# The causal triangle of attention's second pass: from TensorE's sums to a copy on ScalarE, an add on GpSimd and a later exponential

## What is computed

```python
att = jnp.einsum('bthd,bsd->bhts', q, k) * scale
causal = jnp.tril(jnp.ones((Tlen, Tlen), dtype=bool))   # a token sees itself and earlier ones
att = jnp.where(causal[None, None], att, -jnp.inf)
att = jax.nn.softmax(att, axis=-1)
y = jnp.einsum('bhts,bsd->bthd', att, v).reshape(Bsz, Tlen, C)
```

## Time and profile before

| | us |
|---|---|
| median of 3 runs | 1453.11 |
| lowest, highest | 1449.94, 1455.83 |
| the profiled execution, its time | 1456.77 |
| its span, first to last instruction | 1455.5 |
| second passes of attention, from the first exponential to the last weighing | 704 to 1445 |

### The profile page before, as it was taken

One profiled execution on the slowest core, in us unless ns is written; L12 is line 12 of the kernel. 1 busy time (PEld: TensorE's weight loads), 2 busy tenths in 40 slices (PEclk: granted clock), 3 DMA queues, 4 the chain that ended last, 5 costly groups with the idle time before them and its releaser, 6 DMA issues.

```text
span 1455.5 us, 27738 instructions
## 1 busy us (share of the span) xinstructions
PE 1321.3 (91%) x10444; PEld 602.2 (41%) x10444; DVE 1136.2 (78%) x2765; ACT 880.3 (60%) x1177; POOL 498.3 (34%) x449
## 2 busy tenths in 40 slices
PE   5889997898999988789999999999999999999987
PEld 2224232323242323345544455544446545454433
DVE  5698699749887966689888898777886978877734
ACT  2686986687878766432455555555554556455564
POOL 5642453236226241740044340053520254400043
PEclk8799999999999999789999999999999999999998
DMA  7432223222323231565354442254423345533211
GB/s 241 124 117 91 89 90 110 70 93 76 125 83 116 80 103 37 162 169 134 101 145 137 117 122 80 64 139 118 133 80 86 110 126 143 140 93 84 60 46 52
DMA packets 137125, 155.96 MB, mean 107 GB/s; under 512 B 15744, under 2 KB 99456, under 8 KB 136608
## 3 DMA queue, kind: packets, MB, share of 16 engines
q1 hardware_dynamic: 116848, 131.16, 30.7%
q0 software_dynamic: 8192, 16.79, 3.9%
q10 hardware_dynamic: 11952, 6.23, 1.5%
HBM read 109.57 MB, written 44.56 MB: 106 GB/s over the span
## 4 chain that ended last, share of the span: by engine, by line
PE 48%; DVE 10%; ACT 3%; issue 3%; DMA 0%; another core or an unknown queue 0%; POOL 0%; DVEq 0%; ACTq 0%
PE ax_sums L2643 9%; PE second_pair L2680 5%; PE second_pair L2552 5%; PE second_bank L2969 4%; PE second_bank L2939 4%; PE second_pair L2954 4%; ACT ax_prob L2704 2%; DVE am_top L2586 2%; DVE second_pair L2581 2%; PE second_pair L2939 2%; PE second_bank L2954 2%; PE second_pair L2969 2%; PE second_pair L2657 1%; PE first_pair L444 1%; DVE m_hid L3039 1%
## 5 line engine op out<-in xcount | busy, mean ns | idle before, releaser
L2704 ACT ACTIVATE ax_prob<-second_pair 128x1024 f32<-128x1024 f32 (+1 forms) x320 | 295.4, 938 | 220.6 <-PE second_pair L2657 108.9
L476 ACT ACTIVATE m_act_h<-first_pair,const 128x1024 f32<-128x1024 f32 x256 | 272.5, 1116 | 76.9 <-PE first_pair L432 74.6
L2581 DVE CUSTOM_DVE_ANT_0 second_pair<-second_pair,const 128x384 f32<-128x384 f32 (+3 forms) x512 | 238.0, 518 | 51.3 <-PE second_pair L2552 45.6
L2836 POOL DMA_INDIRECT slot_tokens<-xn,mr_slots x128 | 126.3, 987 | 348.1 <-PE second_pair L2969 103.4
L2866 POOL DMA_INDIRECT m_back<-slot_results,mr_slots x128 | 122.9, 960 | 253.3 <-PE second_pair L2657 143.6
L2643 PE MATMUL ax_sums<-ax_prob,al_vs 128*32 128x512 f32 (+3 forms) x1536 | 167.0, 511 | 15.3 <-ACT ax_prob L2704 14.0
L2586 DVE TENSOR_REDUCE am_top<-second_pair 128x2 f32<-128x1024 f32 x128 | 155.3, 1220 | 24.2 <-PE second_pair L2552 21.9
L530 POOL TENSOR_TENSOR m_both<-m_prod,m_both 128x512 f32<-128x512 f32 x64 | 86.5, 1358 | 195.6 <-DVE m_both L491 195.4
L432 PE MATMUL first_pair<-m_terms,w1s 96*128 96x512 bf16 x512 | 148.7, 395 | 5.0 <-ACT m_act_h L476 3.8
L444 PE MATMUL first_pair<-m_act_h,const 128*32 128x512 f32 x1024 | 138.6, 620 | 4.6 <-DVE m_comb L506 1.8
L2680 PE MATMUL second_pair<-al_qs,al_ks 51*128 51x512 bf16 (+3 forms) x768 | 118.5, 337 | 11.1 <-ACT ax_prob L2704 4.9
(11 more groups left out here) (372 smaller groups left out, 2411.6 us busy)
## 6 DMA issues: line engine op xcount, KB each, us to landing
m_wt<-in_experts SPq DMA_DIRECT2D x92, 384.0 KB
m_share<-shares SPq DMA_DIRECT2D x128, 256.0 KB
m_rows<-slot_tokens SPq DMA_DIRECT2D x92, 128.0 KB
slot_results<-m_y SPq DMA_DIRECT2D x92, 128.0 KB
stack<-mp_part SPq DMA_DIRECT2D x48, 128.0 KB
m_terms<-stack SPq DMA_DIRECT2D x64, 96.0 KB, 3.0
qstack<-ap_qpart SPq DMA_DIRECT2D x48, 128.0 KB
al_qs<-qstack SPq DMA_DIRECT2D x32, 192.0 KB, 3.3
```

The lines of the kernel that those rows point to most:

```text
L476: A.activation(self.act_h[:, slot, :, :], banks.bank("up", n, ep)[:, :, :], ACT.Gelu, bias=self.w("b1", 4 * half + ep, 4 * half + ep + 1)) ...
L2581: p = V.tensor_tensor_reduce(tile[:, x, first:first + n], tile[:, x, first:first + n], self.w("later_s", TILE - n, TILE), -1.0, 3e38, ALU. ...
L2704: A.activation(dst, src, ACT.Exp, scale=SCALE).then_inc(*banks.empties("sum", i, u))
```

## The change

The four triangle matmuls go, with their three bf16 constants, the casts, and TensorE's wait for them. On a diagonal step ScalarE now treats the first 128 columns of each head (the corner) apart: it copies them unchanged from PSUM to `ax_prob` and takes the exponential of the others (one instruction more per use, except where n is 128 and the corner is all there is). Then GpSimd adds the fp32 triangle to the corner of all four heads in `ax_prob` (128x512, in place), and ScalarE takes the exponential of it there, in place. The weighing of a diagonal step waits for that. `vector_value` waits for the constants' DMA, as the removed cast did before it in the same queue. The planner's lengths and constants change with it.

```diff
-    def vector_cast(self, loaded, ready):
...
-ATTENTION = 30.17
-SLOTS = [(0, 46.8), (2, 35.51), (9, 36.2), (TASKS, 30.0)]
-FIRST_BLOCK = 32.48
-PACE = 6.11
-FIRST_PACE = 7.33
-DENSE = 28
+ATTENTION = 30.25
+SLOTS = [(0, 47.67), (2, 35.3), (9, 34.93), (TASKS, 30.0)]
+FIRST_BLOCK = 33.66
+PACE = 6.04
+FIRST_PACE = 7.72
+DENSE = 26
...
-            pe("sum", ("sum", i, u), wish, score[n] * len(pairs) + (0.17 if blk >= 4 * th else 0.0), ("maxima", i), lag=0.3, fills=2)
-            act("exp", ("exp", i, u), wish, {384: 0.75, 128: 0.52}.get(n, 0.95), ("sum", i, u),
+            pe("sum", ("sum", i, u), wish, score[n] * len(pairs), ("maxima", i), lag=0.3, fills=2)
+            act("exp", ("exp", i, u), wish, {512: 1.13, 384: 0.92, 256: 1.13, 128: 0.52}[n] if blk >= 4 * th else 0.95, ("sum", i, u),
...
-                pe("weigh", ("weigh", i, m), wish, weighing[n], ("exp", i, u), *front, lag=0.45)
+                if blk >= 4 * th:
+                    pool("mask", ("mask", i, m), 0.0, 1.3, ("exp", i, u), lag=0.15)
+                    act("corner", ("corner", i, m), wish - 20.0, 0.52, ("mask", i, m), lag=0.15)
+                pe("weigh", ("weigh", i, m), wish, weighing[n], ("corner", i, m) if blk >= 4 * th else ("exp", i, u), *front, lag=0.45)
...
+        if (th, blk) in DIAGONALS:
+            e.wait_ge(self.cornered, self.diagonal(i, m) + 1)
...
-                if blk >= 4 * th:
-                    for keys in range(2):
-                        for x in range(2):
-                            p = self.forbid(tile, x, keys, len(pairs) > 1, off)
...
-                A.activation(dst, src, ACT.Exp, scale=SCALE).then_inc(*banks.empties("sum", i, u))
...
+                if (th, blk) not in DIAGONALS:
+                    A.activation(dst, src, ACT.Exp, scale=SCALE).then_inc(*banks.empties("sum", i, u))
+                elif TILE - off == CH:
+                    A.activation(dst, src, ACT.Copy).then_inc(*banks.empties("sum", i, u))
+                else:
+                    A.activation(dst[corner], src[corner], ACT.Copy)
+                    A.activation(dst[plain], src[plain], ACT.Exp, scale=SCALE).then_inc(*banks.empties("sum", i, u))
+
+    def gpsimd_mask(self, loaded):
+        G, g_, banks = self.k.nc.gpsimd, self.k.pool, self.banks
+        later = self.w("earlier_t").unsqueeze(1).broadcast_to([P, HG, CH])
...
+                yield AT["mask", i, m]
+                g_.wait_ge(loaded, 16)
+                for u, (step, _) in enumerate(WEIGHT_USES):
+                    if step == m:
+                        g_.wait_ge(*banks.done("sum", i, u))
+                G.tensor_tensor(self.corner(i, m), self.corner(i, m), later, ALU.add).then_inc(self.masked, 1)
+
+    def scalar_corner(self):
...
+                yield AT["corner", i, m]
+                a_.wait_ge(self.masked, self.diagonal(i, m) + 1)
+                A.activation(self.corner(i, m), self.corner(i, m), ACT.Exp, scale=SCALE).then_inc(self.cornered, 1)
```

55 lines of the change are left out of this document (25 added, 30 removed).

## The result

The kernel after took 1495.2 us (median of 4 runs, 1490.2 to 1503.6), the kernel before on the same chip 1453.0: a ratio of 1.0286, 95% interval 1.0255 to 1.0317. The change makes the kernel 42 us slower; 10 us faster were forecast, with a range to 1466. On a second chip the same pair stands at 1487.3 to 1434.3, 1.0387 (1.0349 to 1.0424).

The account below looks back on a forecast made before the run. TensorE, busy 91% of the span, was taken to bound up to 1391 us, then a chain; -19.9 + 4 + 5 + 1 = -9.9 us takes the median from 1453.1 to 1443, forecast 1437 to 1446, range 1430 to 1466.

Parts of the forecast that it names:

- Shared port: VectorE instructions with only SBUF inputs, hit during GpSimd's masks: 32 us on VectorE, 0 to +3 of time, in the range.
- the sign itself: TensorE before the last expert block: the forecast fails if its idle time there grows by over 10 us.
- The matmuls that go: Triangle matmuls removed from TensorE: 170 uses where it is full give -19.9 us; 22 in the tail count nothing.
- ScalarE's new work: 128 corner exponentials and 160 cut uses raise ScalarE from 415 to about 490 of 745 us: it does not bound.
- The detour: Diagonal weighings follow exponential, mask, corner, about 2.1 us later, mostly covered by other work: +4 us.
- the tail: After the last expert block at 1391, 16 masks share GpSimd's queue with 32 gathers: bounds 0 and +14, taken +5 us.
- the scatters: GpSimd's scatters ahead of phase 2's rows, with masks added among them: nothing to 13 us in each of two phases, taken +1.
- The sign named for the detour: TensorE's waits for ScalarE at the weighings ahead of the last block: under 15 us if the forecast holds, over 30 if (3).
- rival (3): TensorE stands at weighings whose corner is late, so slower; 1473 at 0.3 us a weighing; chance 0.22.
- The last block: Sign at the last expert block: it comes about 15 us earlier than 1391.

Follow-up runs that it names:

- write-only: Kernel after with GpSimd's add replaced by two memsets of a spare tile, same waits, triangle not applied: 1441.0 us, 1.0061.
- both triangles: Kernel after with the four triangle matmuls of each diagonal use put back on TensorE beside GpSimd's additions: 1490.1 us, 1.0401.
- two additions: Kernel after with each 128x512 GpSimd addition made as two of 128x256 that follow each other directly: 1.031.
- even work: Kernel before with 128 additional VectorE operations of 128x192 on a spare tile, one for each diagonal block, for which nobody waits: 1.0044.

## Why the prediction was wrong

**The step that failed** is "Shared port". Its size on VectorE was about right: 32 us estimated, 42 measured over the span (1136.2 to 1178.6). It then put them at "0 to +3 of time", since VectorE "is not full", and left them out of the sum. Even pieces of VectorE's work do cost that little (31 us of busy time for 6). The holds don't come evenly: a join of 0.17 us lasted 2.99, a group of combinations 2.67 in place of 1.14, and VectorE's queue has behind it the maxima for which TensorE is next in line. This step measured +47 us (write-only against after, on two chips of the same speed), not 0 to 3. About half of that is TensorE at 1.2 GHz, in part in stretches that begin just behind such gaps, which the forecast hadn't in its sum at all. The prediction named the sign itself, TensorE idle by over 10 us more ahead of the last block: on the first chip it was 25.5 us before and 60.0 after.

One reading in that step was wrong. Between 584 and 607 us GpSimd wasn't adding: it wrote a tile twice and then issued scatters. The VectorE instruction that lasted 1904 ns is one of the group of four that stood beside the writes:

```profile
584.33 1.80 POOL L2468 MEMSET al_ks<- 32x2048 bf16 x1 [11.09 <-DVEq L54]
584.43 3.73 DVE L1715 TENSOR_SCALAR zt<-x,en_moments,en_roots 128x128 f32<-128x128 f32 x4 [0.22 <-DVEq L54]
586.18 1.84 POOL L2469 MEMSET al_ks<- 32x2048 bf16 x1
```

So this instruction with one tile as input was stretched beside writing alone, while the joins with two inputs were not (176 ns at most in the write-only kernel). The row thus showed a collision, but not the one that the additions were to bring.

**The matmuls that go**: -12 for the whole kernel, not -19.9. Between the first exponential and the last expert matmul, to which the term was confined, the trace has -17, with no more idle time on TensorE than before, so the term was nearly right there, as far as traces of two chips can tell. Why the whole kernel shows only 12 stays open. Beside the held VectorE no gain was seen at all (both triangles: 1.0401 to 1.0387).

**ScalarE's new work** was counted at nothing because 66% is no bound; it costs about 7 us. The 128 exponentials (0.63 us) and the cuts are as forecast.

**The detour, the tail, the scatters**: +4, +5 and +1 stand against +7 for the order and +7 for the way through GpSimd. The sign named for the detour, under 15 us of waits ahead of the last block, holds (5.1 us of waits for ScalarE at the weighings, 1.0 of them for the corners); rival (3) as it was written, with its place at the wait on `cornered`, didn't happen, though its side of the result did. The gathers took 1437.5 to 1493.9, 56 us and in the forecast's 46 to 60. From the last expert matmul to the end there are 1434 to 1502 us, 68, and 64 before (1391 to 1455.5), so the tail grew by 3 to 4, not 5. Phase 2's scatters took 963.3 to 1038.7, 75 us against 58 in the earlier trace rows; the kernel with the new order alone, without a mask, has 69, so most of that came with the order and not with the masks among them. Its rows came at 1040.9, 35 us later than in the earlier trace rows; attention's weighings were 6 to 10 us late by then.

**The last block** came 43 us later than 1391, not 15 earlier. The chances of slower, 0.22, were put on one mechanism; the one that decided was in the text, but priced as VectorE's time instead of as TensorE's waiting.

**What stays open.** Shown: GpSimd's reading is what costs in the kernel after (+47 against writing only, in the same queue with the same waits), and at about the same length of mask reading two operands costs more than reading none (+27). Most of the long holds can go without most of the cost going (two additions), and VectorE's time as such isn't enough (even work). That bursts of held instructions do it is read from timelines, not tested alone. Two things don't fit yet. The same 128 additions cost 12 us up to the last expert matmul where nobody waits for them, in the order of the kernel before, and 41 against writing only where the weighings wait for them. And VectorE's work in the same places without GpSimd cost about 2 us there, for two thirds of the busy time. How much of the rest is the burst's unevenness, how much the order of work and how much GpSimd's own queue, with scatters and gathers behind additions, isn't separated.

## What to carry to other kernels

Work moved to GpSimd was paid here on VectorE, and then by TensorE. So for each GpSimd instruction that reads SBUF, list the VectorE instructions with SBUF inputs only, and follow from each who waits behind it in VectorE's queue; a busy share of 78% was no cover for stalls of 2 to 3 us. Take the GpSimd instruction that reads the least and shortest for the same result (here the select, 0.64 us and one operand: 1.0007 and 1.0006, where the addition stood at 1.0286 and 1.0387, so worth some 40 to 55 us). Have the kernel before measured, and if possible traced, on each chip that an experiment runs on. And don't count what is freed on the fullest engine as time until a version that only removes it has been measured.

## What the runs showed of the hardware

A row of GpSimd additions of 0.44 us each kept a VectorE instruction of 0.17 us waiting for 3.66 us, so the hold wasn't bound to one instruction. With zeros written in between, the longest join was 0.43 us. GpSimd's select of 128x512 took 636 ns against 1281 for its addition and 1492 for adding a constant, and two selects in a row let the joins of VectorE in between (0.65 us at most). Writing only held none of the joins (0.18 us at most). It agrees with the Trainium skill ("SBUF — State Buffer", section "SBUF: two separate sides") that VectorE's two-input instructions are held only against a GpSimd operation that reads SBUF. Some VectorE instructions with one SBUF input were stretched beside writes too: in the write-only kernel a conversion to bf16 of 0.21 us lasted 1.85, and ended when GpSimd's two writes were through:

```profile
L2601 DVE CAST am_part<-am_rows x16: 207/214/1845, 660.1 to 1361.3; 32x128 bf16<-32x128 f32 x16
```

TensorE's clock fell to 1.2 GHz behind such gaps: the same four matmuls took 0.71 us before a gap of 1.88 us and 1.22 us after it.
